# Attention and aggregation over one dense adjacency: the last three pairs of transposed rows made by DMA

## The reference

```
h0 = relu(layernorm(x))
h = h0 @ W_sa;  s_left = h @ a_sa[:256];  s_right = h @ a_sa[256:]
e = where(adj != 0, exp(-leaky_relu(s_left[:, None] + s_right[None, :], 0.01)), 0)
x_a = (e / (sum(e, axis=1) + 1e-5)) @ h
x_b = adj @ (h0 @ W_gcnb) + b_gcnb
attn_a, attn_b = sigmoid([adj @ h0, h0] @ Wa.T + ba), sigmoid([adj @ h0, h0] @ Wb.T + bb)
out = x + sigmoid(attn_a * x_a + attn_b * x_b)
```

## Time and profile before

| what | value |
|---|---|
| median of three runs | 179.38 us (179.19 to 179.73) |
| the profiled execution's own time | 179.66 us |
| its span, first to last instruction | 177.9 us |
| TensorE busy | 172.9 us, 97% of the span |
| VectorE / ScalarE busy | 147.1 us (83%) / 115.3 us (65%) |
| share of TensorE in the chain that ended last | 94% |
| mean granted TensorE clock | 0.990 |

### The profile page before, as it was taken

One profiled execution on the slowest core, in us unless ns is written; L12 is line 12 of the kernel. 1 busy time (PEld: TensorE's weight loads), 2 busy tenths in 40 slices (PEclk: granted clock), 3 DMA queues, 4 the chain that ended last, 5 costly groups with the idle time before them and its releaser, 6 DMA issues.

```text
span 177.9 us, 3403 instructions
## 1 busy us (share of the span) xinstructions
PE 172.9 (97%) x1327; PEld 126.6 (71%) x1327; DVE 147.1 (83%) x309; ACT 115.3 (65%) x169; POOL 18.8 (11%) x42
## 2 busy tenths in 40 slices
PE   7899999999999999999999999999999999999992
PEld 2466677654444458888844488888888888888892
DVE  3779998647999999799999941999999999986552
ACT  3568999752699997838494840575874885763310
POOL 4736346021000200000000000000000000000000
PEclk9969999999999999999999999999999999999999
DMA  5999977999993399000001010000010010011101
GB/s 138 285 235 269 220 125 140 182 199 214 248 423 135 37 214 221 4 4 2 0 4 59 10 49 4 0 0 0 4 59 0 6 59 0 4 61 59 60 32 30
DMA packets 5519, 16.87 MB, mean 95 GB/s; under 512 B 624, under 2 KB 1408, under 8 KB 4736
## 3 DMA queue, kind: packets, MB, share of 16 engines
q0 software_dynamic: 1584, 8.39, 24.5%
q1 hardware_dynamic: 3920, 8.27, 13.1%
HBM read 22.94 MB, written 2.11 MB: 141 GB/s over the span
## 4 chain that ended last, share of the span: by engine, by line
PE 94%; DMA 3%; SPq 1%; DVE 0%; issue 0%; ACT 0%; DVEq 0%
PE ps L772 31%; PE ps L814 16%; PE ps L815 16%; PE ps L813 16%; PE ps L750 7%; PE ps L806 6%; DMA c_sb<-in_consts 3%; PE ps L745 2%; SPq L234 1%; PE ps L873 1%; SPq L239 0%; DVE logit L724 0%; ACT logit L411 0%; DVE res L631 0%; PE ps L855 0%
## 5 line engine op out<-in xcount | busy, mean ns | idle before, releaser
L813 PE MATMUL ps<-mv_lo,e_hi 128*128 128x257 f16 (+2 forms) x272 | 71.0, 267 | 0.0
L815 PE MATMUL ps<-mv_hi,e_lo 128*128 128x257 f16 (+2 forms) x272 | 70.8, 266 | 0.0
L814 PE MATMUL ps<-mv_hi,e_hi 128*128 128x257 f16 (+2 forms) x272 | 70.8, 266 | 0.0
L377 ACT ACTIVATE z<-z,log_e 128x1024 f32<-128x1024 f32 x32 | 36.7, 1146 | 29.1 <-DVE z L568 29.1
L568 DVE SCALAR_TENSOR_TENSOR z<-sl_row,exs,far 128x512 f32<-128x512 f32 x64 | 45.2, 749 | 0.0
L576 DVE TENSOR_TENSOR e_lo<-z,e_hi 128x1024 f16<-128x1024 f32 x32 | 39.1, 1223 | 1.2 <-ACT e_hi L387 1.2
L772 PE MATMUL ps<-adj,nat_lo 128*128 128x512 f16 x128 | 36.8, 379 | 0.0
L772 PE MATMUL ps<-adj,nat_hi 128*128 128x512 f16 x128 | 36.8, 379 | 0.0
L387 ACT ACTIVATE e_hi<-z 128x1024 f16<-128x1024 f32 x32 | 33.3, 1040 | 0.0
L814 PEld LDWEIGHTS ps<-mv_hi,e_hi 128*128 128x128 f16 x272 | 26.5, 98 | 3.2
L813 PEld LDWEIGHTS ps<-mv_lo,e_hi 128*128 128x128 f16 x272 | 26.4, 97 | 3.3
(11 more groups left out here) (69 smaller groups left out, 171.6 us busy)
## 6 DMA issues: line engine op xcount, KB each, us to landing
adj<-in_adj_t POOLq DMA_DIRECT2D x6, 1024.0 KB, 10.4
x_sb<-in_x SPq DMA_DIRECT2D x6, 512.0 KB, 8.9
out<-res SPq DMA_DIRECT2D x7, 256.0 KB, 2.0
adj<-in_adj_t POOLq DMA_DIRECT2D x3, 512.0 KB, 6.7
x_sb<-in_x SPq DMA_DIRECT2D x3, 256.0 KB, 4.7
sl_row<-sl_line SPq DMA_DIRECT2D x1, 768.0 KB, 9.5
adj<-in_adj_t POOLq DMA_DIRECT2D x2, 256.0 KB, 5.6
wa_sb<-in_w_wide SPq DMA_DIRECT2D x1, 258.0 KB, 4.4
```

The costliest lines, as they stand in the source:

```text
L377: act.activation(z[:, n % ZRING, :, :], z[:, n % ZRING, :, :], ACT.Exp, bias=log_e[:, 0:1], scale=SLOPE - 1.0).then_inc(exp_done, 1)
L813: pe.matmul(ps[:, bank, cols], e_hi[:, s, i1], mv_lo[:, j, cols], start=(j == 0), stop=False)
L814: pe.matmul(ps[:, bank, cols], e_hi[:, s, i1], mv_hi[:, j, cols], start=False, stop=False)
L815: return pe.matmul(ps[:, bank, cols], e_lo[:, s, i1], mv_hi[:, j, cols], start=False, stop=(j == NT - 1))
```

## The change

Of the nine units, the last three (pairs 5, 6, 7) are no longer turned on TensorE. SP issues six transposing DMAs instead, a high and a low one for each pair, [128 x 512] float16 from `nat_hi` or `nat_lo` to `h0t_hi` or `h0t_lo`, in an order mixed with the score line's store and spread. The layout of `h0t` becomes tile-major for this. The three wide products move from the front to between pieces of the second chunk's aggregate, and their evictions into steps 2 to 6 of E. The score line is split at tile 8 instead of tile 4. GpSimd issues piece 5 before `norms(6)`, and waits for all six transposing DMAs before it issues pieces 6, 7 and 8. SP waits for them too before the second reading of x.

```diff
-SL_PARTS = ((0, 4), (4, 16))
-SL_UNIT = 4
-SL_BANKS = (2, 0)
+SL_PARTS = ((0, 8), (8, 16))
+SL_UNIT = 5
+SL_BANKS = (6, 0)
+LATE = 3
+ONTIME = NPAIR - LATE
+NTURN = NU - LATE
+WIDE_BANKS = (6, 2, 6, 2, 6, 2, 0, 2)
...
+            def turn_by_dma(p):
+                ts = slice(2 * p, 2 * p + 2)
+                for have, nat, h0t in ((nat_high, nat_hi, h0t_hi), (nat_ready, nat_lo, h0t_lo)):
+                    sp.wait_ge(have, p + 1)
+                    sp.dma_start(h0t[:, ts, :, :].rearrange("p t k n -> p (t k) n"),
+                                 nat[:, ts, :].rearrange("p t d -> p (t d)"),
+                                 transpose=True).then_inc(h0t_landed[p - ONTIME], 16)
+            sp.wait_ge(adj_landed[piece_of(0, NT - 1)], 16)
+            turn_by_dma(ONTIME)
             sl_store(0)
+            turn_by_dma(ONTIME + 1)
             sl_spread(0)
-            sl_store(1)
-            sp.wait_ge(turned, NU)
+            for p in range(ONTIME + 2, NPAIR):
+                turn_by_dma(p)
+            for p in range(ONTIME, NPAIR):
+                sp.wait_ge(h0t_landed[p - ONTIME], 32)
+            sp.wait_ge(turned, NTURN)
...
             norms(5)
+            load_adj(5)
             norms(6)
-            load_adj(5)
             norms(7)
             norms(8)
+            for p in range(ONTIME, NPAIR):
+                pool.wait_ge(h0t_landed[p - ONTIME], 32)
             load_adj(6)
...
+                if n == 2:
+                    mv_highs(5)
+                if n == 3:
+                    mv_highs(6)
+                if n == 5:
+                    mv_highs(7)
...
+                if n == 2:
+                    narrow_results(5)
+                if n == 3:
+                    mv_lows(5)
+                    narrow_results(6)
+                if n == 4:
+                    mv_lows(6)
+                if n == 5:
+                    narrow_results(7)
+                if n == 6:
+                    mv_lows(7)
...
-                if p + 1 < NPAIR:
+                if p + 2 < NTURN:
                     turn(p + 2)
-                wide(p + 1)
-            b_products(1, 0, 4)
-            pe.wait_ge(h0t_ready, NU)
+                if p + 1 < NTURN:
+                    wide(p + 1)
+            b_products(1, 0, 8)
+            wide(6)
+            b_products(1, 8, 12)
+            pe.wait_ge(h0t_ready, NTURN)
+            wide(7)
+            b_products(1, 12, 16)
+            wide(8)
+            b_products(2, 0, 4)
             sl_lines(1)
-            b_products(1, 4, 16)
-            b_products(2, 0, 16)
+            b_products(2, 4, 16)
```

More of the change, by code:

```diff
@@ L119, in build @@
         e_lo = sb("e_lo", [P, 2 * ESLOT, CW], F16)
-        h0t_hi = e_hi[:, 16:24, :].rearrange("p (k s) n -> p k (s n)", k=KT)
-        h0t_lo = e_lo[:, 16:24, :].rearrange("p (k s) n -> p k (s n)", k=KT)
+        h0t_hi = e_hi[:, 16:24, :].rearrange("p s (a k n) -> p (s a) k n", k=KT, n=P)
+        h0t_lo = e_lo[:, 16:24, :].rearrange("p s (a k n) -> p (s a) k n", k=KT, n=P)
         zeros = e_hi[:, 0, :]
@@ L136, in build @@
         part_b = sb("part_b", [P, 2, D], F32)
-        sl_turn = [part_b[0:hi - lo, h, 0:P] for h, (lo, hi) in enumerate(SL_PARTS)]
+        sl_turn = [c_sb[0:hi - lo, C_WT + h * P:C_WT + (h + 1) * P] for h, (lo, hi) in enumerate(SL_PARTS)]
         gated_b = sb("gated_b", [P, 2, 2, D], F32)
@@ L172, in build @@
         h0t_ready = sem("h0t_ready")
+        h0t_landed = [sem(f"h0t_landed{p}") for p in range(ONTIME, NPAIR)]
         wide_product = sem("wide_product")
@@ L219, in turn_bank, with h0t_tiles @@
             n = (UNITS[u][1] - UNITS[u][0]) * P
-            return ps[:, u % 2, 0:KT * n].rearrange("p (k n) -> p k n", k=KT)
-        def h0t_cols(tile, u):
-            return tile[:, :, UNITS[u][0] * P:UNITS[u][1] * P]
+            return ps[:, u % 2, 0:KT * n].rearrange("p (t k n) -> p t k n", k=KT, n=P)
+        def h0t_tiles(tile, u):
+            return tile[:, UNITS[u][0]:UNITS[u][1], :, :]
         def wide_bank(t):
-            return WIDE_BANKS[t // 2 % 2] + t % 2
+            return WIDE_BANKS[t // 2] + t % 2
         block = ctx.enter_context(nc.Block())
@@ L268, in _ @@
                 sp.dma_start(x_sb[:, ts, :], x[:, ts, :]).then_inc(x_back[g], 16)
+            sl_store(1)
             sl_spread(1)
@@ L431, in _ @@
                     nat_highs(p + 2)
-                mv_highs(p)
-            act.activation(factor_l[:, :], exs[:, :, SL], ACT.Exp, scale=SLOPE).then_inc(factors_done, 1)
+                if p < ONTIME:
+                    mv_highs(p)
             agg_highs(0)
-            sl_lines(1)
             act.wait_ge(wg_landed, 16)
@@ L442, in _ @@
                     act_high(n - 1)
-                if n in (2, 3, 4):
-                    half_added(n - 2)
+                if n == 2:
[4 more added lines that the diff above has]
+                    mv_highs(7)
+                    act.activation(factor_l[:, :], exs[:, :, SL], ACT.Exp, scale=SLOPE).then_inc(factors_done, 1)
+                if n in (4, 7, 8, 9):
+                    half_added((4, 7, 8, 9).index(n))
                 if n == 6:
                     agg_highs(1)
-                    half_added(3)
+                    sl_lines(1)
                 if n == 10:
@@ L562, in dve_z @@
                 if j == 0:
-                    dve.wait_ge(sl_ready[min(c, 1)], 16)
+                    dve.wait_ge(sl_ready[c // 2], 16)
                 if n >= ZRING:
@@ L654, in _ @@
                     nat_lows(p + 1)
-                if p > 1:
+                if 1 < p <= ONTIME:
                     mv_lows(p - 1)
@@ L658, in _ @@
                     moments(p + 4)
-                narrow_results(p)
-                if p + 1 < NPAIR:
+                if p < ONTIME:
+                    narrow_results(p)
+                if p + 2 < NTURN:
                     h0t_lows(p + 2)
-            mv_lows(NPAIR - 1)
             agg_lows(0)
@@ L743, in turn @@
                     for k in range(KT):
-                        cols = slice((t - UNITS[u][0]) * P, (t - UNITS[u][0] + 1) * P)
-                        ins = pe.transpose(turn_bank(u)[:, k, cols], x_sb[:, t, k * P:(k + 1) * P], ident[:, :])
+                        ins = pe.transpose(turn_bank(u)[:, t - UNITS[u][0], k, :], x_sb[:, t, k * P:(k + 1) * P], ident[:, :])
                 ins.then_inc(turned, 1)
@@ L754, in wide @@
             def wide(u):
-                pe.wait_ge(h0t_ready, u + 1)
+                if u < NTURN:
+                    pe.wait_ge(h0t_ready, u + 1)
+                else:
+                    pe.wait_ge(h0t_landed[u - NTURN], 32)
                 if u == 1:
```

11 lines of the change are left out of this document (5 added, 6 removed).

## The result

The changed kernel takes 188.14 us (median of 6 runs, 187.44 to 188.90) where the kernel before takes 179.35 (178.79 to 179.91): a ratio of 1.051 [1.0477, 1.0543], some 9 us slower. I had forecast slower, by 3.5 us, because TensorE would wait for adjacency piece 6. It does wait there, but the loss is more than twice as large. The profiled execution took 187.91 us with a span of 186.1, against 179.66 and 177.9 before: 8.2 us to explain.

The account below looks back on a forecast made before the run. TensorE was taken to bound the kernel (busy 172.9 of 177.9 us). Piece 6, issued at 36.9, lands 8.8 later at 45.7, 3.5 us past the break-even of 42.2: 179.38 + 3.5 = 182.9 us, range 181.0 to 191.9.

Parts of the forecast that it names:

- The range: Forecast kernel time with TensorE waiting for piece 6 and the clock kept: 181.0 to 191.9 us around 182.9.
- break-even 33.4: GpSimd's queue: piece 6 must be issued by 33.4 us for the attention products to start no later than before.
- TensorE at row tile 8: Second aggregate on TensorE: row tile 8 reached at about 41.5 us; starting that part at 42.2 would break even.
- The transposing DMA: SP's queue: 1.5 us each for issue and data, one after another; the last lands at 36.9 us.
- The upper bound: Price of one transposing DMA on SP's queue: 512 packets, 32 on each of 16 engines, at 95 ns: 3.0 us.
- The landing of piece 6: GpSimd's adjacency piece: issued at 36.9, takes 8.8 us, not 7.6, beside x's second reading; lands at 45.7 us.
- The forecast (TensorE waits for piece 6, clock kept): TensorE before row tile 8 of the second aggregate: waits 4.2 us, attention products 3.5 us later, 182.9 us; chance 0.47.
- the fall: Rival, TensorE behind its wait: the clock falls too and 1.7 us more are lost, +5.2, 184.6 us; chance 0.23.
- All this is hidden: Early piece 5, evictions moved into E (3.4 us on VectorE) and later score line half cost nothing; slack 5 us.
- Never waiting: Rival: TensorE never waits for piece 6 and keeps 0.7 to 1.0 us, 178.6 us; chance 0.10.
- the draw: Rival: piece 6 lands at 42 to 42.5 us, about when TensorE needs it, 179.4 us; chance 0.08.

Follow-up runs that it names:

- Experiment 2: Changed kernel with SP's second reading of x (2 MB) waiting until piece 6 has landed: 184.77 us, 1.0324 of the kernel before.
- experiment 6: Changed kernel with piece 6 issued ahead of GpSimd's wait and SP's second reading of x behind piece 6: 182.12 us, 1.0215 of the kernel before.
- experiment 7: Kernel of experiment 6 with the last wide product and the second score line put later on TensorE: 184.63 us, 1.0379 of the kernel before.
- experiment 10: Kernel of experiment 7 with x's second reading held until piece 8 has landed and half additions at E's steps 7 to 10: 179.37 us, 1.002.
- experiment 3: Changed kernel with 32 unused 512-column matmuls on TensorE just before it needs piece 6: 185.69 us, 1.0382 of the kernel before.
- Experiment 5: Changed kernel with x's second reading behind piece 6 and 20 unused matmuls filling TensorE's wait: 182.46 us, 1.0224 of the kernel before.
- experiment 4: Changed kernel with all nine units turned on TensorE, no transposing DMAs or waits for them, its other edits kept: 183.40 us, 1.0284 of the kernel before.
- experiment 12: Kernel of experiment 10 with piece 7 waiting only for the transposing DMAs of pairs 5 and 6, piece 8 for all: 178.55 us, 0.9973.
- experiment 11: Kernel of experiment 10 with pieces 6 and 7 both issued ahead of the wait for the transposing DMAs: 180.79 us, 1.0135 of the kernel before.
- experiment 1: Changed kernel without GpSimd's wait for the six transposing DMAs before pieces 6, 7 and 8: 191.88 us, 1.073 of the kernel before.

## Why the prediction was right in kind and wrong in size

Direction and mechanism were right: each place named was found, with the releaser named. The size was off: 3.5 us forecast, some 8.8 measured in the medians and 8.2 in the profiles. The range held the time, near its upper part. Step by step:

| step | forecast | measured |
|---|---|---|
| last transposing DMA landed | 36.9 | 36.05 |
| piece 6 issued (break-even 33.4) | 36.9 | 36.62 |
| TensorE at row tile 8 | 41.5 | 40.40 |
| piece 6, issue to landing | 8.8 | 11.43 |
| piece 6 landed | 45.7 | 48.05 |
| TensorE waits | 4.2 | 7.70 |
| clock behind the wait | kept | 2.3 lost |
| attention products begin | 69.2 | 73.89 |

*The transposing DMA.* I took 1.5 us for each on SP's queue from bounds of 0.3 and 3.0, and measured are 1.20 to 2.00, with 3.4 to 4.2 us to land. The upper bound had the count of packets nearly right (512) and the price of one wrong: SP's queue has 7184 packets where it had 3920, 544 more for each DMA, and the time that they took rose from 13.1% of 177.9 us to 16.5% of 186.1, which is some 36 ns each and not 95 (an estimate); 34 on each engine are then 1.2 us. The step held, and with it the claim on which the sign rested, that piece 6 could not be issued by 33.4. The two prices from the Trainium skill in the forecast are both off here: 0.5 us (an estimate) by the page "DMA: Bandwidth & Descriptors", section "Latency and other measured facts", and 5.2 us (an estimate) by "VectorE: DVE Perf Modes", section "The three transpose paths". The measurement decides.

*TensorE at row tile 8.* 1.1 us earlier than forecast. About 1.05 of it is the early stretch whose clock was 0.50 in the profile of before and 1.00 in this one. This changes the wait but not the end, since the wait ends when piece 6 lands.

*The landing of piece 6: the first step that failed*, "so I take 8.8 and not 7.6". I saw the right collision, that SP's second reading of x is released at the same moment, and then took the price of another: the 8.8 us of the earlier trace rows had the 256 KB spread of the score line beside them, not 2 MB. It was 11.43. Experiment 2 takes the reading away and the piece takes 7.55; experiments 6 and 7 give it back to piece 7 (11.30 and 11.22), and experiment 10 takes it away there too (7.47). From the landing, +2.6 us less 0.3 for the earlier issue is +2.3 at the start of the attention products.

*The clock: the second step that failed.* "The forecast (TensorE waits for piece 6, clock kept)" had 0.47, and the fall stood among the rivals with 0.23. The trace shows the fall behind the wait, and experiment 3 shows that it costs 2.3 us (I had 1.7). The section "HAM oscillation" of the Trainium skill's page "TensorE: Matmul & The Clock Gate" has the lower clock come back after a long idle gap. The trace agrees: 0.50 behind the 7.70 us. I had the row (0.50 behind small gaps) and gave a longer gap the smaller chance. Both errors together are 2.3 + 2.3 = 4.6, the 4.7 by which the attention products came later than forecast. Experiment 5 undoes both and comes to 182.46.

*"All this is hidden", the other edits.* It came true in the changed kernel, for a reason that I had not worked out. I costed E by the end of its eighth step, while the places that TensorE can wait for are the evictions amid E's steps. In experiment 4, where E starts at 41.77 because the spread lands late, TensorE waits 1.5 and 1.9 us for them, and 4.7 us come out. What keeps them hidden in the changed kernel is its early E, at 35.67, together with TensorE's own wait. Whether the early E alone would do, no run shows. An estimate from experiment 6 says that it just would: there the last `exs` comes 16.7 us behind the start of E (55.82 against 39.15), that is 52.3 + 0.2 = 52.5 for a start at 35.67, and TensorE, going on at 40.40 without a wait, would want it at 40.40 + 3 x 3.45 + 2 x 1.33 = 53.4.

*Never waiting and the draw.* Neither came. With x's reading out of the way of the pieces, experiments 10 and 12 come to a draw; there the transposing DMAs still meet piece 6.

So the 1.3 us of work do leave TensorE, and are lost to waits. Not because the DMA engines were full: over the stretch in which the six DMAs run, 24.0 to 36.1 us, the mean DMA share was 0.88 (0.85 in the same stretch before), and from 30 to 32 us it was 0.33. Held back by the program, the adjacency leaves DMA time unused there; let go, it makes the transposes and the spread late, and whatever waits for them: the next piece, E, or TensorE. The two are bound by a choice of order, and none of the orders tried here wins. That no other order does was not shown, nor was a kernel with fewer bytes of adjacency to move.

## What to carry over

Where work moves from the bounding engine to the DMA queues, price what it makes late there: write for each transfer what else is in flight between its issue and its landing, with its bytes, and take the landing of a row that had as many bytes beside it. A wait that is forecast on TensorE is to be charged with the slower clock behind it as well, unless the trace shows a wait as long without it. And an edit that only moves work is to be costed at the places where the bounding engine waits for it, with the start that its chain really has: the late evictions cost nothing here with E from 35.67, and 3.4 us of TensorE's waits with E from 41.77.

## What the runs showed of the hardware

- A transposing DMA of [128 x 512] float16 kept SP 1.2 to 2.0 us for its issue in the changed kernel, where a plain one took 0.3 to 0.6. Beside one 1 MB adjacency piece in flight the issue was 2.33 us and the landing 7.07 (experiment 6), and an issue of 3.30 us occurred (experiment 12); the piece took 8.0 to 8.8 beside them (experiments 1, 6, 7 and 10), and 10.4 in the profile of experiment 12. Beside two or three it was 7.10 and 8.66, and landings reached 18.7 us (experiments 11 and 1).
- The 1 MB adjacency piece took 7.5 to 7.6 us from issue to landing with little beside it (experiments 2 and 10), 8.8 with 256 KB, and 11.2 to 11.4 beside 2 MB of x, three times alike (the changed kernel, experiments 6 and 7).
- The granted clock fell to 0.50 behind the 7.7 us wait and to a mean of 0.65 over 3.15 us behind one of 2.96 us, and did not behind one of 2.87 us; other executions of that same kernel (experiment 6) had a mean granted clock of 0.987 and 0.989, so no bound can be drawn between the two waits. 32 unused matmuls in the wait of 7.7 us kept it at the full level (experiment 3).
